# Perceiver layer on one core: low halves of the keys subtracted on GpSimd, layer norm vectors loaded as rows

## What is computed

```python
def layer_norm(x, gamma, beta):
    mu = jnp.mean(x, axis=-1, keepdims=True)
    var = jnp.mean(jnp.square(x - mu), axis=-1, keepdims=True)
    return (x - mu) * jax.lax.rsqrt(var + EPS) * gamma + beta

xn = layer_norm(_layernorm(x), g_x, b_x)         # 32 x 32 x 512
cn = layer_norm(context, g_c, b_c)               # 32 x 257 x 384
q, k, v = heads(xn @ Wq), heads(cn @ Wk), heads(cn @ Wv)     # 16 heads of 64
x = x + (softmax(q @ k.T / 8) @ v) @ Wo
x = x + self_attention(_layernorm(x), W_qkv, W_o)            # 16 heads of 32
x = x + layer_norm(sum over the two best experts of p * (gelu(_layernorm(x) @ w1 + b1) @ w2 + b2))
```

## Time and profile before

| | |
|---|---|
| runs | 1573.94, 1579.29, 1582.66 us |
| median | 1579.29 us |
| profiled execution, its own time | 1575.59 us |
| its span | 1574.0 us (mean granted TensorE clock 0.981) |
| start until q_proj | 0 to 24.07 us |
| groups 0 to 7 | to about 780 us |
| body(8), routing, first experts | to about 832 us |
| 23 expert jobs, then the last norm | to 1574 us |

### The profile page before, as it was taken

How to read it: one execution, slowest core, us unless ns; L and a number is a source line. 1 busy time by engine, 2 the same in 40 slices (tenths; PEclk the granted TensorE clock), 3 DMA queues, 4 the chain that set the end, 5 groups by cost and what they waited for, 6 DMA issues and landing times.

```text
span 1574.0 us, 22638 instructions
## 1 busy us (share of the span) xinstructions
PE 1472.5 (94%) x7708; PEld 913.7 (58%) x7709; DVE 679.8 (43%) x1822; ACT 448.8 (29%) x916; POOL 114.0 (7%) x167
## 2 busy tenths in 40 slices
PE   3899999999999999999965999999999999999997
PEld 3668686686866769677552444444444444444442
DVE  2764747657476674765533312112112212212215
ACT  1553626445263452625401111111111111111100
POOL 1000010000100101010011000000000000000005
PEclk9999999999999999999976999999999999999997
DMA  8680000000000010000056251606051346000005
GB/s 276 229 303 2 31 24 10 30 13 30 23 18 22 13 32 22 20 23 12 1 214 236 105 225 68 240 13 260 20 214 59 121 152 260 14 19 20 13 7 167
DMA packets 42784, 140.25 MB, mean 89 GB/s; under 512 B 4792, under 2 KB 4792, under 8 KB 37632
## 3 DMA queue, kind: packets, MB, share of 16 engines
q0 software_dynamic: 16256, 83.89, 14.0%
q1 hardware_dynamic: 24640, 55.93, 10.5%
q10 hardware_dynamic: 1856, 0.01, 0.1%
HBM read 110.46 MB, written 29.36 MB: 89 GB/s over the span
## 4 chain that ended last, share of the span: by engine, by line
PE 80%; DVE 11%; issue 3%; ACT 2%; DMA 2%; POOL 1%; ACTq 0%; SPq 0%; DVEq 0%; POOLq 0%
PE bank L546 20%; PE bank L564 20%; PE bank L1199 7%; PE bank L1240 6%; PE bank L1162 4%; PE bank L1265 4%; PE bank L1183 3%; PE bank L1253 3%; PE bank L556 3%; PE bank L1287 2%; PE bank L1321 2%; PE bank L1222 2%; DMA ccol<-in_L_xattn_b_c_dram 1%; DVE mx L945 1%; DVE cstats L915 1%
## 5 line engine op out<-in xcount | busy, mean ns | idle before, releaser
L546 PE MATMUL bank<-moe_w,arena 128*128 x736 | 332.4, 595 | 2.3 <-POOL pool_mark L354 2.3
L564 PE MATMUL bank<-moe_w,arena 128*128 x736 | 330.9, 592 | 0.0
L458 DVE TENSOR_TENSOR arena<-bank,arena 128x512 f32<-128x512 f32 x92 | 63.7, 692 | 478.5 <-PE bank L546 478.5
L546 PEld LDWEIGHTS bank<-moe_w,arena 128*128 128x128 f32 x736 | 140.3, 191 | 178.7 <-issue 178.7
L396 ACT ACTIVATE arena<-arena 128x512 f32<-128x512 f32 x92 | 57.9, 630 | 578.6 <-DVE arena L458 578.6
L564 PEld LDWEIGHTS bank<-moe_w,arena 128*128 128x128 f32 x736 | 132.7, 190 | 132.5 <-issue 132.5
L1199 PE MATMUL bank<-moe_w 128*128 128x257 f32 x768 | 188.4, 382 | 2.4 <-DVE moe_w L765 2.4
L1240 PE MATMUL bank<-moe_w 86*128 86x512 f16 (+1 forms) x576 | 153.4, 379 | 5.1 <-ACT moe_w L821 3.3
L1199 PEld LDWEIGHTS bank<-moe_w 128*128 128x128 f32 x768 | 137.2, 190 | 21.8 <-DVE moe_w L765 2.6
L807 ACT ACTIVATE moe_w<-bank,ccol,ugain 128x512 f32<-128x512 f32 x96 | 74.6, 778 | 92.8 <-PE bank L1240 91.9
L962 DVE TENSOR_TENSOR moe_w<-bank,moe_w 86x512 f16<-86x512 f32 (+1 forms) x96 | 64.5, 685 | 69.7 <-ACT moe_w L821 69.5
(11 more groups left out here) (188 smaller groups left out, 1595.4 us busy)
## 6 DMA issues: line engine op xcount, KB each, us to landing
moe_w<-in_L_ffn_w_dram POOLq DMA_DIRECT2D x16, 4096.0 KB, 19.4
xs_rows<-blocks SPq DMA_DIRECT2D x8, 2048.0 KB, 13.8
arena<-in_ctx_dram SPq DMA_DIRECT2D x32, 382.5 KB
arena<-in_L_ffn_b_dram POOLq DMA_DIRECT2D x8, 1024.0 KB, 26.7
arena<-xs_rows SPq DMA_DIRECT2D x23, 256.0 KB, 2.7
ys_rows<-arena SPq DMA_DIRECT2D x23, 256.0 KB, 2.0
moe_w<-in_L_xattn_Wq_dram SPq DMA_DIRECT2D x1, 2048.0 KB, 9.7
moe_w<-in_L_xattn_Wo_dram SPq DMA_DIRECT2D x1, 2048.0 KB, 21.8
```

The lines of the kernel that those rows point to most:

```text
L458: nc.vector.tensor_tensor(h_sb[:, fb % 2, :], bank[fb % 2][:, :], b1_rows[:, bass.ds(slot * FF + fb * 512, 512)], ALU.add).then_inc(h_bias ...
L546: last = nc.tensor.matmul(bank[fb % 2][:, :], xsT[:, k, :], moe_flat[:, bass.ds((e % 2) * 16384 + k * FF + fb * 512, 512)], start=(k == 0) ...
L564: last = nc.tensor.matmul(Y[:, :], hT_sb[:, fb % 2, c, :], moe_flat[:, bass.ds((e % 2) * 16384 + 8192 + (4 * fb + c) * DIM, DIM)], start=( ...
```

## The change

`n_lo` moves from DVE to POOL. So that it is a plain subtraction, `cn_stats` multiplies the variance by `N_SCALE ** -2`, which makes the normalised context come out with its factor of 2048; `n_hi` becomes a copy, and `ct_out` takes the gain divided by 2048 (`cgain`, one more small instruction at the start). The four layer norm vectors are loaded as 14 rows of 128 values into the place of `y2`; PE transposes them once into bank 7, ACT copies the 14 columns to `cols`.

```diff
--- before.py
+++ after.py
@@ -148,9 +148,12 @@
         before = sb("before", [P, P])
         ones = sb("ones", [P, P])
         gate = sb("gate", [P, KD, EXPERTS])
-        gcol = sb("gcol", [P, 2, KD])
-        ccol = sb("ccol", [P, 2, KC])
+        cols = sb("cols", [P, 2 * KD + 2 * KC])
+        gcol = cols[:, 0:2 * KD].rearrange("p (k c) -> p k c", k=2)
+        ccol = cols[:, 2 * KD:2 * KD + 2 * KC].rearrange("p (k c) -> p k c", k=2)
+        col_rows = y2[0:2 * KD + 2 * KC, 0:P]
         ugain = sb("ugain", [P, KC])
+        cgain = sb("cgain", [P, KC])
         gate_bias = sb("gate_bias", [P, EXPERTS])
         half = sb("half", [P, 8])
         stats = sb("stats", [P, 6])
@@ -240,6 +243,7 @@
         x0_in = sem("x0_in")
         x_in, wk_in, wq_in, wv_in, wo_in = sem("x_in"), sem("wk_in"), sem("wq_in"), sem("wv_in"), sem("wo_in")
         qkv_in, wos_in, cols_in, rows_in, gate_in = sem("qkv_in"), sem("wos_in"), sem("cols_in"), sem("rows_in"), sem("gate_in")
+        cols_full, cols_ok = sem("cols_full"), sem("cols_ok")
         ctx_in = [sem(f"ctx_in{b}") for b in range(GB)]
         xs_zeroed = sem("xs_zeroed")
         consts, ident_ok, zeros_ok, memset_ok = sem("consts"), sem("ident_ok"), sem("zeros_ok"), sem("memset_ok")
@@ -691,18 +695,33 @@
                 pool.wait_ge(cn_var, n + 1)
                 nc.gpsimd.tensor_tensor(crstd[0:86, :], cmv[0:86, :, 1], half[0:86, 0:3], ALU.pow).then_inc(cn_rstd, 1)
 
+            def n_lo(g, b):
+
+                pool.wait_ge(n_high_done, GB * g + b + 1)
+                for k in range(3):
+                    last = nc.gpsimd.tensor_tensor(n_low[0:PART[k], b, k, :], ctx[0:PART[k], b, k, :],
+                                                   n_high[0:PART[k], b % 2, k, :], ALU.subtract)
+                last.then_inc(n_low_done, 1)
+
             def body(g, do_a, do_b, nxt):
                 ln = ln_before(g)
                 if nxt:
                     ln_pow(ln)
                 if do_b:
                     mark_free(g - 1)
+                if do_a:
+                    n_lo(g, 0)
                 if isinstance(g, int) and g == 0:
                     cn_pow(2)
                 if do_a:
+                    n_lo(g, 1)
                     cn_pow(GB * g + 3)
+                    n_lo(g, 2)
                 if nxt:
                     cn_pow(GB * g + 4)
+                if do_a:
+                    n_lo(g, 3)
+                if nxt:
                     cn_pow(GB * g + 5)
                     cn_pow(GB * g + 6)
                     ln_pow(ln + 1)
@@ -767,13 +786,15 @@
 
         @block.scalar
         def _(act):
-            with nc.allow_non_contiguous_dma(reason="a few columns"):
-                act.dma_start(gcol[:, 0, :], g_x.rearrange("(c p) -> p c", p=P)).then_inc(cols_in, 16)
-                act.dma_start(gcol[:, 1, :], b_x.rearrange("(c p) -> p c", p=P)).then_inc(cols_in, 16)
-                act.dma_start(ccol[:, 0, :], g_c.rearrange("(c p) -> p c", p=P)).then_inc(cols_in, 16)
-                act.dma_start(ccol[:, 1, :], b_c.rearrange("(c p) -> p c", p=P)).then_inc(cols_in, 16)
-            act.wait_ge(cols_in, 64)
+            act.dma_start(col_rows[0:KD, :], g_x.rearrange("(c p) -> c p", p=P)).then_inc(cols_in, 16)
+            act.dma_start(col_rows[KD:2 * KD, :], b_x.rearrange("(c p) -> c p", p=P)).then_inc(cols_in, 16)
+            act.dma_start(col_rows[2 * KD:2 * KD + KC, :], g_c.rearrange("(c p) -> c p", p=P)).then_inc(cols_in, 16)
+            act.dma_start(col_rows[2 * KD + KC:, :], b_c.rearrange("(c p) -> c p", p=P)).then_inc(cols_in, 16)
+            act.wait_ge(cols_full, 1)
+            nc.scalar.copy(cols[:, :], BK[:, 0:2 * KD + 2 * KC]).then_inc(cols_ok, 1)
+            act.wait_ge(cols_ok, 1)
             nc.scalar.activation(ugain[:, :], ccol[:, 0, :], ACT.Identity, scale=1.0 / (N_SCALE * P_SCALE)).then_inc(ugain_ok, 1)
+            nc.scalar.activation(cgain[:, :], ccol[:, 0, :], ACT.Identity, scale=1.0 / N_SCALE).then_inc(ugain_ok, 1)
 
             def xn_out(n):
 
@@ -787,7 +808,7 @@
 
                 act.wait_ge(tp_full, n + 1)
                 nc.scalar.activation(cnT[:, b % 2, c, :], TP[:, 0:KEYS], ACT.Identity,
-                                     bias=ccol[:, 1, c:c + 1], scale=ccol[:, 0, c:c + 1]).then_inc(tp_free, 1)
+                                     bias=ccol[:, 1, c:c + 1], scale=cgain[:, c:c + 1]).then_inc(tp_free, 1)
 
             def m_copy(g, at, dst, src):
                 act.wait_ge(m_full, M_FILLS * g + at + 1)
@@ -811,7 +832,7 @@
 
                 act.wait_ge(cn_done, GB * g + b + 1)
                 for k in range(3):
-                    last = nc.scalar.activation(n_high[0:PART[k], b % 2, k, :], ctx[0:PART[k], b, k, :], ACT.Identity, scale=N_SCALE)
+                    last = nc.scalar.copy(n_high[0:PART[k], b % 2, k, :], ctx[0:PART[k], b, k, :])
                 last.then_inc(n_high_done, 1)
 
             def pt_hi(g, b, k):
@@ -919,7 +940,7 @@
                 for k in range(3):
                     last = nc.vector.bn_aggr(cmv[0:PART[k], k, :], cstats[0:PART[k], k, :])
                 link(last)
-                nc.vector.tensor_scalar(cmv[0:86, :, 1], cmv[0:86, :, 1], EPS, None, ALU.add).then_inc(cn_var, 1)
+                nc.vector.tensor_scalar(cmv[0:86, :, 1], cmv[0:86, :, 1], EPS, N_SCALE ** -2, ALU.add, ALU.mult).then_inc(cn_var, 1)
 
             def cn_apply(g, b):
 
@@ -961,15 +982,6 @@
                 src, _, _, emptied = pt_place(g, b, k)
                 nc.vector.tensor_tensor(pT_low[0:PART[k], k, :], src[0:PART[k], :], pT_high[0:PART[k], k, :],
                                         ALU.subtract).then_inc(emptied, 1)
-
-            def n_lo(g, b):
-
-                dve.wait_ge(n_high_done, GB * g + b + 1)
-                for k in range(3):
-                    last = nc.vector.scalar_tensor_tensor(out=n_low[0:PART[k], b, k, :], in0=ctx[0:PART[k], b, k, :],
-                                                          scalar=N_SCALE, in1=n_high[0:PART[k], b % 2, k, :],
-                                                          op0=ALU.mult, op1=ALU.subtract)
-                last.then_inc(n_low_done, 1)
 
             def heads_apart(g):
 
@@ -1018,8 +1030,6 @@
                     dve.wait_ge(x_in, 16)
                 if nxt:
                     xn_norm(ln, g + 1, 0)
-                if do_a:
-                    n_lo(g, 0)
                 for b in range(GB):
                     ahead = (do_a and b == 1) or (nxt and b >= 2)
                     if do_a:
@@ -1027,8 +1037,6 @@
                             if b >= 1 and k < 3:
                                 pt_lo(g, b - 1, k)
                             row_max(g, b, k)
-                    if do_a and b > 0:
-                        n_lo(g, b)
                     if ahead:
                         cn_stats(g, b + 2)
                     if do_a:
@@ -1400,6 +1408,8 @@
                     rk_fill(g - 1)
 
             pe.wait_ge(ident_ok, 1)
+            pe.wait_ge(cols_in, 64)
+            nc.tensor.transpose(BK[:, 0:2 * KD + 2 * KC], col_rows, ident[0:2 * KD + 2 * KC, 0:2 * KD + 2 * KC]).then_inc(cols_full, 1)
             xn_fill(0, 2)
             pe.wait_ge(wq_in, 16)
             body(0, True, False, True)
```

## The result

| | before | with the change |
|---|---|---|
| median of 20 runs each | 1579.17 us | 1573.74 us |
| ratio, 95% interval | | 0.9962 (0.9954 to 0.9971) |
| profiled execution, span | 1575.59, 1574.0 us | 1574.32, 1572.6 us |

The kernel became 0.38% faster, 6 us by the ratio, which is half of the 11.8 us that the forecast had. One of the 20 runs of before took 2642.85 us, and one run of experiment 5 took 1705.92 us; both are runs of a slow state and in no ratio.

A forecast was written before the change was run, and what follows sets the result against it. PE was taken as the bound, busy 1472.5 of 1574.0 us. From 1579.3 us, 11.8 won at the start and 0 for the low halves gave 1567.5 us; the range was 1563 to 1584.

The forecast's parts named there:

- rival 1: At heads_apart, POOL holds off one or two DVE copies: 0.3 to 1.2 us per body, result 1570 to 1576; chance 0.12.
- Term 1: At the start, vectors loaded as rows let q_proj begin at 12.3 instead of 24.07 us: 11.8 us won.
- rival 4: At the start, late loads catch PE: W_o by 3.6 us, or zero writes 2 and W_o 1.6; 1571 to 1575; chance 0.08.
- The reading of the DMA windows: At 12 to 16 us, 217 GB/s blamed on 4 byte runs; without them later loads land up to 1.6 us earlier.
- Term 2: In the loop, moving the low halves' subtractions from DVE to POOL gains and costs nothing: 0 us.
- POOL's price: One low-half subtraction on POOL takes 0.87 us, 2.6 us for a batch, with 1.0 and 5.2 as ends.
- the room for `crstd`: In batch 3, POOL's three subtractions fit before crstd is wanted at 189.1 us: room 6.5 us, 2.2 per instruction.
- 0.34 in all: Chances of POOL and DVE blocking: in part 0.12, in full 0.12, in full with slower POOL 0.10.
- Rival 2: At heads_apart, each of three subtractions delays a copy: DVE 2.6, PE 2.1 us late per body, 1585 us; chance 0.12.
- The side case in body(0): In body(0), cn_apply of context 2 meets the same three POOL subtractions: up to 2.6 us more lost.
- The argument I set against it: At heads_apart, DVE's four copies, if first and without gaps, finish by 154.0 and POOL merely runs 1.7 us later.

The follow-up runs named there:

- experiment 5: The change, with two of POOL's three subtractions of a batch merged into one instruction of 768 columns: 1574.02 us, ratio 0.9977.
- experiment 1: The change with only the vectors as rows, the low halves subtracted on DVE as before: 1567.29 us, ratio 0.9928 against the kernel before.
- experiment 3: The change, with POOL's subtractions of batch 1 waiting until heads_apart is over (in body(0), until context 2 is normalised): 1566.39 us, ratio 0.9923.
- experiment 4: The change, with heads_apart written as a maximum over an axis of length 1 instead of a copy: 1566.63 us, ratio 0.9924.
- experiment 6: experiment 3 plus seven unread identity transposes in each of the two gaps between the transposes of context 0: 1563.50 us, ratio 0.9910.
- experiment 7: experiment 6 plus unread identity transposes earlier on PE, 25 and 6 ahead of xn_fill and 10 ahead of q_proj: 1563.19 us, ratio 0.9908.
- experiment 2: The change with only the subtractions on POOL, the vectors loaded in 4 byte runs as before: 1585.46 us, ratio 1.0043 against the kernel before.

## Why the prediction was right, and where it was not

The range held the time and the direction was right, but the forecast, 1567.5 us, was 6 us too low. The time came out in the range of rival 1, to which I had given a chance of 0.12. The range held because it took in the rivals, not because the account of the low halves was right.

- **Term 1, 11.8 us at the start: the mechanism right, the exact agreement luck.** `q_proj` moved by 12.4 us, and experiment 1, which has only this term, is 11.8 us under the 1579.08 us of its own before. Two sizes within it were off: the first rows of x landed 0.7 us earlier than before (2.9 us after their issue, not 3.6), which made the start of `q_proj` 0.7 us better than forecast, and TensorE took 2.3 us more in body(0) (1.7 of them the lower clock at L1150), which no step of mine had. So the trace of experiment 1 has only 10.5 us of gain left at body(1). No load was late, W_o landed at 24.4 us: rival 4 didn't come.
- **The reading of the DMA windows was wrong.** I took the 217 GB/s of 12 to 16 us for the work of the 4 byte runs. The same dip is there without them: 222 GB/s at a share of 1.02 in 10 to 14 us of the changed kernel. Wk, W_qkv and W_o did land 1.6 to 1.8 us earlier, but the dip wasn't gone; what makes it is open.
- **Term 2, the low halves at no cost: this step failed.** That less work on DVE brings PE nothing was right (experiment 3 against 1), and so was POOL's price, 0.91 us against 0.87, and the room for `crstd`. DVE's busy time fell by only 24.9 us with the change (679.8 to 654.9), not by 47, since its lengthened instructions took part of it back; in experiment 3 it fell by 39.1. What failed was to count the meeting with `heads_apart` at nothing and give it 0.34 in all. It came in every body from body(1) on, at 0.96 us of PE's time in the loop, and `cn_apply`'s cost 1.8 us in body(0).
- **Rival 1, its mechanism right and its size at the upper end.** I had 0.3 to 1.2 us a body, by one or two copies held off for 0.87 us each. Three were held off, for 0.63 us each, as the copies and POOL's instructions overlap in part: DVE was 1.87 us late (3.57 against 1.70) and PE 0.96 us. Rival 2 had the right number of copies and too high a price for each. That DVE had a further 0.23 us of idle time to give was in the trace and left out.
- **The side case in body(0)**, `cn_apply` against the same triple, was worth 1.78 us where rival 2 had up to 2.6.
- **The rule.** The Trainium skill, SBUF — State Buffer, section "Who interferes with whom", says that GpSimd and a VectorE instruction in a two-port mode exclude each other for a whole instruction, and that one with a single SBUF input outside these modes is free of it. Experiments 5 (1772 ns) and 4 (676 ns beside POOL) agree with both halves. The size is a little smaller than a whole instruction: a copy and a subtraction together took 1.04 us, not 0.41 + 0.91. The argument I set against it, that DVE's four copies would keep their turn if they were first, is refuted: the first copy ran in 0.42 us, and each of the next three came after one of POOL's.

The time saved by the medians, 5.4 us, is more than the 1.4 us of the two spans. The sums of the bodies explain the spans; the other 4 us are not explained by the two terms. They go for the most part with the mean granted clock of a run. Of the 27 timings of the kernel before made beside the experiments, the six at 0.981 or 0.982 took 1574.05 to 1575.98 us, and the 21 at 0.976 to 0.980 took 1576.24 to 1582.75. With the change the four at 0.981 or 0.982 took 1571.32 to 1571.81 us, the 16 at 0.978 to 0.980 up to 1574.44. At the same clock the gain is thus about 3 us. Why one execution has more of the low clock than another is open. A difference of 2 or 3 us between two medians here is therefore no proof by itself.

## What to carry to other kernels

Before work is moved to GpSimd, look at what VectorE does in the same microseconds: here the fast copies from SBUF to SBUF (512 columns in 0.41 us) and the fast normalisations (384 columns in 0.47 us) were held off by each GpSimd subtraction and held it off in turn. `pt_lo` and `row_max`, which read PSUM, were not (675 to 690 and 407 to 427 ns for every one of them), and neither was the maximum that stood in for the copy. Where the moved work has room, a wait that puts it behind such an instruction costs a line and gives the loss back (experiment 3). And a vector of a few hundred values is loaded in rows and turned by one transpose: 1856 packets of 4 bytes kept the first matmuls of `q_proj` back by 12 us.

## What the runs showed of the hardware that I had not expected

- The turns are strict: copy, subtraction, copy, subtraction, with one copy per 1.04 us, less than 0.42 + 0.91 us. So it seems that a GpSimd instruction doesn't hold DVE off for all of the duration that its row shows.
- The granted clock of TensorE fell to 0.50 within 26 to 30 us in all five kernels with the early start and no filling (the change, experiments 1, 3, 4 and 5), right after a thin stretch of PE (0.6 to 0.9 us busy in 24 to 26). With seven unused transposes in each of two gaps of under a microsecond it stayed at 1.00 (experiments 6 and 7, one profile each). In the two kernels with the late start, before and experiment 2, the same gaps, at 36 to 38 us, were not followed by a fall; why is open. Another low stretch follows in every kernel after a wait of PE of 2.3 to 2.5 us for copies out of PSUM, with the change at 38 to 40 us (0.50), before at 48 to 52 (0.59 and 0.56), and the filling left it in place.
